# Graph attention with running sums in SBUF, no DMA in the edge loop but the gathers, and the sums first in each of TensorE's slots

## The chip, the cores and the metric

The kernel runs on one core of one Trainium2 chip. The metric is the time of the program on the device in microseconds (us), the median of some runs. All times of the profile come from one profiled execution.

## The reference

The inputs are 6250 nodes of 256 features and 200000 edges; `dst` is sorted, and since it is drawn as 6250 times the square of a uniform number, the edges are dense at low nodes and thin at high ones. Cut to what matters:

```python
# graph attention on xn = layernorm(x)
proj = (xn @ Wp.T).reshape(-1, 8, 32)
s = sum(proj * a_src)[src] + sum(proj * a_trg)[dst]
s = leaky_relu(s, 0.2)
s = s - max(s)
exp_s = exp(s)
denom = segment_sum(exp_s, dst)
out = segment_sum(proj[src] * exp_s / (denom[dst] + 1e-16), dst)
x = x + elu(out + xn @ Wskip.T + bias)
# top-2 of 8 experts with a hidden width of 1024, on layernorm(x)
x = x + sum over the two experts of weight * (gelu(xe @ W1 + b1) @ W2 + b2)
```

## The kernel before

The program has six stages, one after the other: `edge_tables` (indices of the edges turned so that an edge lies on each partition), `node_phase` (normalized, projected rows of all nodes, written to a table in DRAM), `edge_phase` (the edge loop, which this change is about), `route_phase` (attention output, router, tokens scattered by expert), `expert_phase` and `combine_phase`.

**The edge loop.** The sorted edges are taken in sub-tiles of 128, 4 sub-tiles in a **set** (512 edges), 2 sets in a **step**. There are 392 sets: 98 iterations of a loop body with 4 sets, u = 0 to 3. All edges of a step go to a window of 128 nodes that starts at the step's first target (`base_tab`). Where a step spanned more, the whole loop would be run once more (`over_passes`); with these inputs there is one pass. A **slot** is what each engine does for one set. For set u:

- GpSimd gathers, in four indirect DMAs (`rows[k]`, line 555), the table row of each edge's source: 256 projected features, 8 source scores, 8 target scores.
- VectorE compares (line 625): it writes `onehot[k]`, for each edge the one-hot row of its node in the window.
- TensorE turns the one-hots (`turn`, four fp32r matmuls against an identity, line 574), ScalarE copies them from PSUM (`onehot_t`, line 714), and TensorE multiplies them with the target scores of the window's nodes (`target_scores`, four fp32 matmuls of 9 columns, line 582). This gives each edge its target's score in the bank `z[k]`; the ninth column, of ones, tells which edges are in the window.
- VectorE adds source and target score (`add`, lines 634 and 637), ScalarE takes the exponential twice: as a factor in PSUM (line 718) and into the last 8 columns of `weighed`. VectorE multiplies the gathered rows by the factor (`weigh`, line 643).
- TensorE sums over edges by node (`sums`, four fp32 matmuls of one-hots by `weighed`, 264 columns, line 592) into a PSUM bank that is shared by the two sets of a step. After the step VectorE adds the bank to `accbuf` (`accumulate`, line 659).

A matmul of fp32 operands is issued as two instructions, so `sums` is 8 and `target_scores` 8, `turn` 4.

**The running sums** lie in DRAM (`acc_rows`). For each step SyncE loads the 128 rows of its window into `accbuf`, and stores them when the step has been added. A window's load waits for the store of the one before, as the windows overlap. SyncE also loads the window's 128 by 8 target scores (`st_w`) out of the table. `acc_rows` is cleared in the first stage and read again in `route_phase`.

**What sets the order.** No scheduler: each engine runs the instructions in the order in which its own function is written, and semaphores connect them. TensorE's slot u is `turn(u+2)`, `sums(u)`, `target_scores(u+2)`; VectorE's is `add(u)`, `weigh(u)`, `compare(u+2)`, then `accumulate` or `largest` (the running maximum of the exponentials, lines 650 and 654); ScalarE's is the exponentials of u, the copy of the indices, and `copy_turned(u+2)`. There are 4 buffers of rows, one-hots, `weighed` and `z`, and one bank for the turned one-hots. A gather into `rows[k]` waits for the weighing of the set before in the same buffer (`weigh_done[k]`).

## Time and profile before

| what | value |
| --- | --- |
| median of 3 runs | 3961.45 us (3962.35, 3954.32, 3961.45) |
| profiled execution, its own time | 3958.48 us |
| profiled execution, span | 3956.9 us |
| granted clock of TensorE, mean | 0.735 of full speed |
| TensorE (PE) busy | 2792.9 us, 71% |
| weight loads (PEld) busy | 2407.7 us, 61% |
| VectorE (DVE) busy | 1816.3 us, 46% |
| GpSimd (POOL) busy | 1746.9 us, 44% |
| ScalarE (ACT) busy | 874.4 us, 22% |

The span is from the first to the last recorded instruction. Busy shares are means over all stages: by the windows of the trace the edge loop is from about 227 to 2811 us, 65% of the span; the stage of tables ends at about 30 us, routing at about 3158 us. A matmul's end is modelled in the records: a TensorE instruction can be drawn as ended while the engine that waits for it goes on waiting.

### The profile page before, as it was taken

The numbers are of one execution on the slowest core, as the hardware profiler recorded it, in microseconds if no ns is written. First come the engines' busy times: TensorE is split into PE (matmuls) and PEld (weight loads), VectorE is DVE, ScalarE is ACT, GpSimd is POOL, SyncE is SP. The second block draws the span as 40 slices with busy tenths as digits, with TensorE's granted clock in tenths as the row PEclk, the third lists the DMA queues.
The fourth block names the chain that finished last, engine by engine and source line by source line (L and its number), as shares of the span: only waits on it lengthen the run. The fifth ranks groups of instructions, "written<-read, shape, count | busy, mean of one in ns | idle before, by whom it ended". The sixth has DMA issues, their size and how long they took to land. (4 is left out here: it accounts for less than half of the span.)

```text
span 3956.9 us, 52520 instructions
## 1 busy us (share of the span) xinstructions
PE 2792.9 (71%) x14065; PEld 2407.7 (61%) x14066; DVE 1816.3 (46%) x4809; ACT 874.4 (22%) x2715; POOL 1746.9 (44%) x1828
## 2 busy tenths in 40 slices
PE   5766777687777777777787778777303439999991
PEld 4445666566666656666666667566302339999991
DVE  5533434343443333343344434343576546666654
ACT  2211111111111111111111111111101225555540
POOL 0045555555555555555555556555103632221210
PEclk8977767766776776777767666667655569999995
DMA  4333333333333333333333334333332242221216
GB/s 149 113 104 104 106 105 108 102 109 103 105 105 105 106 108 106 106 103 109 104 109 108 107 107 110 101 104 106 95 114 64 68 121 68 66 86 45 65 45 200
DMA packets 256279, 400.63 MB, mean 101 GB/s; under 512 B 76674, under 2 KB 187739, under 8 KB 255625
## 3 DMA queue, kind: packets, MB, share of 16 engines
q0 software_dynamic: 98560, 262.95, 24.2%
q1 hardware_dynamic: 138165, 117.93, 9.7%
q10 hardware_dynamic: 19540, 19.60, 1.5%
q8 instruction: 4, 0.07, 0.0%
q14 instruction: 10, 0.08, 0.0%
HBM read 318.49 MB, written 81.71 MB: 101 GB/s over the span
## 5 line engine op out<-in xcount | busy, mean ns | idle before, releaser
L555 POOL DMA_INDIRECT rows<-proj_table,idx x1568 | 1482.2, 945 | 1312.7 <-DVE weighed L643 548.3
L592 PE MATMUL banks<-weighed,onehot 128*128 128x264 f32 x3136 | 1186.1, 543 | 0.0
L592 PEld LDWEIGHTS banks<-weighed,onehot 128*128 128x128 f32 x3136 | 827.3, 277 | 177.8
L582 PEld LDWEIGHTS banks<-st_w,onehot_t 128*128 128x128 f32 x3152 | 550.9, 254 | 618.1 <-ACT onehot_t L714 435.5
L582 PE MATMUL banks<-st_w,onehot_t 128*128 128x9 f32 x3152 | 534.6, 298 | 494.8 <-ACT onehot_t L714 383.3
L643 DVE TENSOR_TENSOR weighed<-rows,banks 128x1024 f32<-128x1024 f32 x392 | 478.7, 1221 | 560.8 <-ACT banks L718 370.7
L714 ACT COPY onehot_t<-banks 128x512 f32<-128x512 f32 x394 | 230.9, 586 | 2143.3 <-remote 1418.3
L574 PE MATMUL banks<-ident_r,onehot 128*128 128x128 f32 x1576 | 355.4, 364 | 146.9 <-DVE onehot L625 99.4
L634 DVE TENSOR_TENSOR raw_score<-rows,banks 128x32 f32<-128x32 f32 x392 | 73.1, 186 | 730.2 <-remote 501.5
L574 PEld LDWEIGHTS banks<-ident_r,onehot 128*128 128x128 f32 x1576 | 296.1, 264 | 168.5 <-DVE onehot L625 114.5
L1368 POOL DMA_INDIRECT results_by_token<-yrow,goes_to x104 | 108.6, 1044 | 479.2 <-DVE yrow L1316 350.1
L625 DVE SCALAR_TENSOR_TENSOR onehot<-banks,base_tab,dst_tab 128x512 fp32r<-128x512 f32 x394 | 293.5, 745 | 0.0
L1255 ACT ACTIVATE hid<-banks,params 128x256 f32<-128x256 f32 x416 | 198.0, 478 | 268.0 <-PE banks L1211 261.5
L1211 PE MATMUL banks<-f_xth,w1h 128*128 128x256 f32 x832 | 236.2, 284 | 28.5 <-ACT hid L1255 14.6
L1110 POOL DMA_INDIRECT tokens_by_expert<-r_xn,slot x100 | 118.1, 1181 | 278.8 <-issue 233.7
L1304 DVE TENSOR_TENSOR hidl<-hid,hidh 128x256 fp32r<-128x256 f32 x416 | 169.9, 424 | 149.4 <-ACT hidh L1249 138.3
L1211 PE MATMUL banks<-f_xth,w1l 128*128 128x256 f32 x832 | 234.1, 281 | 0.0
L1211 PE MATMUL banks<-f_xtl,w1h 128*128 128x256 f32 x832 | 234.0, 281 | 0.0
L659 DVE TENSOR_TENSOR accbuf<-accbuf,banks 128x264 f32<-128x264 f32 x197 | 83.8, 425 | 242.5 <-remote 198.5
L1211 PEld LDWEIGHTS banks<-f_xth,w1h 128*128 128x128 f32 x832 | 158.2, 190 | 32.5 <-issue 16.4
L1224 PE MATMUL banks<-w2h,hidh 128*128 128x256 f32 x832 | 170.4, 286 | 0.0
L1224 PE MATMUL banks<-w2l,hidh 128*128 128x256 f32 x832 | 166.1, 281 | 0.0
(214 smaller groups left out, 2860.6 us busy)
## 6 DMA issues: line engine op xcount, KB each, us to landing
accbuf<-acc_rows SPq DMA_DIRECT2D x197, 132.0 KB
acc_rows<-accbuf SPq DMA_DIRECT2D x197, 132.0 KB
rows<-proj_table,idx POOLq DMA_INDIRECT x1568
w_raw<-in_L_ffn_W_dram POOLq DMA_DIRECT2D x16, 1024.0 KB
xrow<-tokens_by_expert SPq DMA_DIRECT2D x106, 128.5 KB
c_y<-results_by_token SPq DMA_DIRECT2D x10, 1120.0 KB
proj_table<-trow ACTq DMA_DIRECT2D x50, 132.8 KB
acc_rows<-clear SPq DMA_DIRECT2D x5, 1320.0 KB, 13.1
```

What stands on the lines that cost most here:

```text
L555: nc.gpsimd.indirect_dma_start(rows[k][:, i, :], None, table, bass.IndirectOffsetOnAxis(ap=idx[k][:, i:i + 1], axis=0)).then_inc(gathered[ ...
L574: mm = nc.tensor.matmul(turn_bank[:, i * P:(i + 1) * P], onehot[k][:, i, :], m["ident_r"][:], start=True, stop=True)
L582: mm = nc.tensor.matmul(z[k][:, i, :], onehot_t[k % 2][:, i * P:(i + 1) * P], st_w[k // 2][:], start=True, stop=True)
L592: mm = nc.tensor.matmul(acc_bank[k // 2][:, 0:ROW], onehot[k][:, i, :].bitcast(F32), weighed[:, k * SET + i, :], start=(k % 2 == 0 and i = ...
L625: nc.vector.scalar_tensor_tensor(onehot[k][:], node_row.unsqueeze(1).to_broadcast(shape), m["base_tab"][:, bass.ds(2 * it + ahead // 2, 1) ...
L643: nc.vector.tensor_tensor(weighed[:, k * SET:(k + 1) * SET, 0:D].rearrange("p s (h f) -> p s h f", h=H), rows[k][:, :, 0:D].rearrange("p s ...
L714: nc.scalar.copy(onehot_t[k % 2][:], turn_bank[:]).then_inc(turn_copied[k], 1)
L1110: nc.gpsimd.indirect_dma_start(xg, bass.IndirectOffsetOnAxis(ap=slot[u][k][:], axis=0), xn[:, u, k, :], None).then_inc(sent[u], 16)
L1211: mm = nc.tensor.matmul(h_bank[j % HB][:, 0:TOK], w[:, s, k, at], v[:, k, :], start=(k == 0 and n == 0), stop=(k == KD - 1 and n == 2))
L1224: mm = nc.tensor.matmul(y_bank[h][:, 0:D], v[:, j, h * P:(h + 1) * P], w[:, s, j, :], start=(j == 0 and n == 0), stop=(j == JH - 1 and n = ...
L1255: nc.scalar.activation(hid[:, j, :], h_bank[j % HB][:, 0:TOK], ACT.Gelu, bias=params[:, s, B1 + j:B1 + j + 1]).then_inc(h_ready[j % HB], 1)
L1304: nc.vector.tensor_tensor(hidl[:, j, :], hid[:, j, :], hidh[:, j, :].bitcast(F32), ALU.subtract).then_inc(hid_low, 1)
```

## The change

The sums and the target scores stay in SBUF for the whole loop.

- `acc` is now a tile of 125 partitions by 52 node tiles by 264 columns, zeroed by GpSimd in the first stage. Windows are 125 nodes wide, so a window touches two neighbouring node tiles. `accumulate` (line 751) makes two VectorE instructions for a step: the bank times a 0/1 column (`upper`) added to the one node tile, and times the other column (`nextt`) to the next one. Which tile, a table says (`tile_int`), from which VectorE reads 7 registers in an iteration.
- Target scores are kept as three bf16 parts of 8 columns in `st_parts`, made at the end of `node_phase`. `pick` (lines 705 and 708) puts the 24 columns of a window together in two VectorE instructions for each step; `target_scores` is four bf16 matmuls of 24 columns (line 647), and a new VectorE instruction, `reduce` (line 713), adds the three parts of each score from PSUM to SBUF.
- `turn` (line 637) reads the upper halves of the fp32 one-hots as bf16, so it is four bf16 matmuls; there are two turn banks, two `z` banks, four `onehot_t` and eight `onehot`.
- `compare` (line 695) needs one table in place of two: `key_tab`, each edge's place in the window, is worked out ahead for all edges in the first stage (`find_keys`), with `inside_tab`, which says which edges are in the window and takes the place of the column of ones.
- An iteration has 8 sets, so there are 49. TensorE's slot u is now `sums(u)`, `turn(u+4)`, `target_scores(u+2)`. VectorE's is `add(u)`, `reduce(u+1)`, `pick` (even u) or `accumulate` (odd u), `compare(u+5)`, `weigh(u)`, and `largest` (odd u). ScalarE copies set u+3.
- The table's rows are 264 words long, not 272. The DRAM buffer `acc_rows`, its clearing, all of SyncE's loads and stores in the loop, and the loads of the sums in `route_phase` are gone. After a pass `next_windows` works out the keys of the next pass (`find_keys` again), even after the last one.

```diff
-SET, K = 4, 4
+SET = 4
 G = 2 * SET
+ROUND = 8
+STEPS_A_ROUND = ROUND * SET // G
+BUF = 4
...
-STEPS = 2 * -(-NSUB // (2 * G))
-IT = STEPS // 2
+STEPS = STEPS_A_ROUND * -(-NSUB // (STEPS_A_ROUND * G))
+IT = STEPS // STEPS_A_ROUND
+AHEAD = 3
...
-TROW = ROW + H
-ZC = H + 1
-ACC_TILES = -(-(N + P) // P)
...
+PARTS = 3
+ZC = PARTS * H
...
-            acc=sb("acc", [NP, NT, ROW]), neg_bound=sb("neg_bound", [P, 1]),
+            acc=sb("acc", [NP, NT + 2, ROW]), neg_bound=sb("neg_bound", [P, 1]),
...
+def find_keys(nc, m, step, settle):
+    def by_step(t):
+        return t[:, 0:(STEPS + AHEAD) * G].rearrange("p (s g) -> p s g", g=G)
+    key, inside = m["key_tab"], m["inside_tab"]
+    step(nc.vector.tensor_tensor(by_step(key), by_step(m["dst_tab"]),
+                                 m["base_tab"][:].unsqueeze(2).to_broadcast([P, STEPS + AHEAD, G]), ALU.subtract))
+    settle()
+    step(nc.vector.tensor_scalar(inside[:], key[:], 0.0, None, ALU.is_ge))
+    settle()
+    step(nc.vector.scalar_tensor_tensor(inside[:], key[:], float(NP), inside[:], ALU.is_lt, ALU.mult))
+    settle()
+    step(nc.vector.scalar_tensor_tensor(key[:], m["place_tab"][:], 1.0, inside[:], ALU.add, ALU.mult))
...
+            nc.gpsimd.memset(m["acc"][:], 0.0)
...
+            for to, op in ((m["upper"], ALU.is_le), (m["nextt"], ALU.is_gt)):
+                step(nc.vector.tensor_scalar(to[:, 1:1 + STEPS + AHEAD], first[:], m["iota_p"][:], None, op))
+                step(nc.vector.tensor_scalar(to[:, 0:1], first[:, STEPS - 1:STEPS], m["iota_p"][:], None, op))
...
+            targets = m["dst_tab"][:, 0:(STEPS + AHEAD) * G]
+            whole_parts(m["inside_tab"][:], targets, m["key_tab"][:])
...
+            step(nc.vector.scalar_tensor_tensor(m["place_tab"][:], m["inside_tab"][:], -float(NP), targets,
+                                                ALU.mult, ALU.add))
+            find_keys(nc, m, step, settle)
...
+            parts = [m["st_parts"][0:NP, 0:NT, q * H:(q + 1) * H] for q in range(PARTS)]
+            nc.vector.tensor_copy(parts[0], st_all[:]).then_inc(st_step, 1)
+            dve.wait_ge(st_step, 1)
+            nc.vector.tensor_tensor(st_rest[:], st_all[:], parts[0], ALU.subtract).then_inc(st_step, 1)
+            dve.wait_ge(st_step, 2)
+            nc.vector.tensor_copy(parts[1], st_rest[:]).then_inc(st_step, 1)
+            dve.wait_ge(st_step, 3)
+            nc.vector.tensor_tensor(parts[2], st_rest[:], parts[1], ALU.subtract)
...
-        onehot, onehot_t = tiles("onehot", [P, SET, P], F32R), tiles("onehot_t", [P, SET * P], n=2)
...
+        onehot, onehot_t = tiles("onehot", [P, SET, P], n=ROUND), tiles("onehot_t", [P, SET * P], BF16)
+        onehot16 = [o[:].bitcast(BF16).rearrange("p s (e half) -> p s e half", half=2)[:, :, :, 1] for o in onehot]
+        ident16 = sb("ident16", [P, P], BF16)
...
+            def turn(s, copied, compared):
+                if copied is not None:
+                    pe.wait_ge(turn_copied[(s - 2) % BUF], copied)
+                pe.wait_ge(onehot_ready[s % BUF], compared)
                 for i in range(SET):
...
+                    mm = nc.tensor.matmul(turn_bank[s % 2][:, i * P:(i + 1) * P], onehot16[s % ROUND][:, i, :],
+                                          ident16[:], start=True, stop=True)
+                mm.then_inc(turned[s % BUF], 1)
+            def target_scores(s, count, read):
+                pe.wait_ge(turn_copied[s % BUF], count)
+                pe.wait_ge(st_ready[s // 2 % 2], count)
+                if read is not None:
+                    pe.wait_ge(reduced[(s - 2) % BUF], read)
                 for i in range(SET):
...
+                pe.wait_ge(weigh_done[k], weighed_count)
                 for i in range(SET):
...
+                    mm = nc.tensor.matmul(acc_bank[u // 2 % 2][:, 0:ROW], onehot[u][:, i, :],
+                                          weighed[:, k * SET + i, :], start=(u % 2 == 0 and i == 0),
+                                          stop=(u % 2 == 1 and i == SET - 1), skip_group_check=True)
                 mm.then_inc(sum_done[k], 1)
...
-                for u in range(K):
-                    ahead = (u + 2) % K
-                    turn(ahead, now if u < 2 else nxt)
-                    sums(u, now, nxt)
-                    target_scores(ahead, now if u < 2 else nxt, now16 if u < 2 else nxt16)
...
+                at = counts(pe, c, 3)
+                for u in range(ROUND):
+                    sums(u, at(u), at(u + 4))
+                    turn(u + 4, at(u + 2), at(u + 4))
+                    target_scores(u + 2, at(u + 2), at(u))
...
+            def compare(s, it, free):
+                if free is not None:
+                    dve.wait_ge(sum_done[s % BUF], free)
                 shape = [P, SET, P]
...
+                nc.vector.tensor_tensor(
+                    onehot[s % ROUND][:], node_row[s % 2].unsqueeze(1).to_broadcast(shape),
+                    m["key_tab"][:, bass.ds(ROUND * SET * it + s * SET, SET)].unsqueeze(2).to_broadcast(shape),
+                    ALU.is_equal).then_inc(onehot_ready[s % BUF], 1)
+            def pick(s, it, tile_of, count):
+                q, b = s % 2, s % BUF
+                col = STEPS_A_ROUND * it + 1 + s
+                st = [m["st_parts"][:, bass.ds(t, 1), :].rearrange("p a k -> p (a k)") for t in (tile_of, tile_of + 1)]
+                nc.vector.tensor_scalar(st_pick[q][:], st[1], m["nextt"][:, bass.ds(col, 1)], None, ALU.mult
+                                        ).then_inc(st_picked[q], 1)
+                dve.wait_ge(st_picked[q], count)
+                nc.vector.scalar_tensor_tensor(st_w[b][:], st[0], m["upper"][:, bass.ds(col, 1)], st_pick[q][:],
+                                               ALU.mult, ALU.add).then_inc(st_ready[q], 1)
+            def reduce(s, count):
+                dve.wait_ge(z_ready[s % BUF], count)
+                nc.vector.tensor_reduce(target[s % BUF][:], z_parts[s % 2], X, ALU.add).then_inc(reduced[s % BUF], 1)
...
+            def accumulate(q, col, tile_of, summed, before):
                 dve.wait_ge(sum_done[2 * q + 1], summed)
...
+                dve.wait_ge(acc_added[1 - q], before)
+                for side, t in ((m["upper"], tile_of), (m["nextt"], tile_of + 1)):
+                    to = m["acc"][:, bass.ds(t, 1), :].rearrange("p a d -> p (a d)")
+                    ins = nc.vector.scalar_tensor_tensor(to, acc_bank[q][0:NP, 0:ROW], side[0:NP, bass.ds(col, 1)], to,
+                                                         ALU.mult, ALU.add)
+                ins.then_inc(acc_added[q], 1)
...
+                at = counts(dve, c, 4)
+                landed = [value_of(dve, 16 * SET * (2 * it + q + 1)) for q in range(2)]
+                tile_of = tiles_of_steps(STEPS_A_ROUND * it, 7)
+                for u in range(ROUND):
+                    add(u, at(u), landed[u // BUF])
+                    reduce(u + 1, at(u + 5))
                     if u % 2:
...
+                        accumulate((u - 3) // 2 % 2, STEPS_A_ROUND * it + (u - 1) // 2, tile_of[(u - 1) // 2],
+                                   at(u + 2), at(u - 1))
                     else:
...
+                        pick(u // 2 + 2, it, tile_of[u // 2 + 3], at(u + 4))
+                    compare(u + 5, it, at(u + 1))
+                    weigh(u, at(u))
+                    if u % 2:
+                        largest(u, it, at(u), at(u + 1))
...
+            def copy_turned(s, count):
+                act.wait_ge(z_ready[s % BUF], count)
+                act.wait_ge(turned[s % BUF], count)
+                nc.scalar.copy(onehot_t[s % BUF][:], turn_bank[s % 2][:]).then_inc(turn_copied[s % BUF], 1)
...
-                    sp.wait_ge(z_ready[2 * j + 1], now)
-                    load_scores(j, ahead)
-                    sp.wait_ge(acc_added[1 - j], nxt if j else now)
-                    store(1 - j, done)
-                    sp.wait_ge(acc_stored, value_of(sp, 16 * (2 * c + j + 1)))
-                    load(j, here)
...
```

TensorE in the body of the edge loop, slot 0 before; `banks` are PSUM banks, and "x3" stands for the three matmuls that follow the first with the same operands:

```order
L574 MATMUL banks<-ident_r,onehot2 128x128 [waits onehot_ready2]
L574 MATMUL banks<-ident_r,onehot2 128x128 x3
L592 MATMUL banks<-weighed,onehot0 128x264 [waits weigh_done0,exp_ready0,acc_added0]
L592 MATMUL banks<-weighed,onehot0 128x264 x3
L582 MATMUL banks<-st_w1,onehot_t0 128x9 [waits st_loaded1,turn_copied2]
L582 MATMUL banks<-st_w1,onehot_t0 128x9 x3
```

The same slot of TensorE with the change:

```order
L658 MATMUL banks<-weighed,onehot0 128x264 [waits weigh_done0,exp_ready0,acc_added0]
L658 MATMUL banks<-weighed,onehot0 128x264 x3
L637 MATMUL banks<-ident16,onehot4 128x128 [waits onehot_ready0,turn_copied2]
L637 MATMUL banks<-ident16,onehot4 128x128 x3
L647 MATMUL banks<-st_w1,onehot_t2 128x24 [waits reduced0,st_ready1,turn_copied2]
L647 MATMUL banks<-st_w1,onehot_t2 128x24 x3
```

The turn has moved behind the sums, and is for the set four ahead; the scores are still those of the set two ahead, behind the same sums.

VectorE in the same body, before, from the accumulation of slot 0 to the end of slot 1:

```order
L659 TENSOR_TENSOR accbuf1<-accbuf1,banks 128x264 [waits acc_loaded1,sum_done3]
L634 TENSOR_TENSOR raw_score1<-rows1,banks 128x32 [waits gathered1,z_ready1]
L636 REGISTER_ALU
L637 SCALAR_TENSOR_TENSOR score1<-raw_score1 128x32 [waits added]
L643 TENSOR_TENSOR weighed<-rows1,banks 128x4x256 [waits factor_ready1]
L625 ISA [waits sum_done3]
L625 SCALAR_TENSOR_TENSOR onehot3<-banks,base_tab,dst_tab 128x512
L650 TENSOR_TENSOR masked<-weighed,banks 128x64 [waits exp_ready1]
L654 TENSOR_TENSOR runmax<-runmax,masked 128x64 [waits maxed]
```

And VectorE's slot 1 with the change:

```order
L719 TENSOR_TENSOR raw_score1<-rows1,target1 128x32 [waits gathered1,reduced1]
L722 SCALAR_TENSOR_TENSOR score1<-raw_score1 128x32 [waits added1]
L713 TENSOR_REDUCE target2<-banks 128x32 [waits z_ready2]
L751 ISA [waits acc_added0,sum_done3]
L751 SCALAR_TENSOR_TENSOR acc<-banks,upper,acc 125x264
L751 ISA
L751 SCALAR_TENSOR_TENSOR acc<-banks,nextt,acc 125x264
L695 ISA [waits sum_done2]
L695 TENSOR_TENSOR onehot6<-banks,key_tab 128x512
L729 TENSOR_TENSOR weighed<-rows1,banks 128x4x256 [waits factor_ready1,sum_done1]
```

The weighing of set 1 was the third instruction of its slot and waited for set 1's own scores alone; now the reduction of set 2, with its wait for set 2's scores (`z_ready2`), the accumulation and the comparison stand ahead of it in VectorE's queue.

## Rows read from the trace of the kernel before

**Rows 1.** Windows by stage: us, then each engine's busy us (instructions), granted clock, DMA share, GB/s

```profile
227.00:2796.00 2569.00, 1927.52 (x7778) 1606.14 (x7779) 1019.93 (x2144) 430.41 (x1563) 1481.35 (x1568) 0.70 0.39 106
2811.00:3158.00 347.00, 78.01 (x372) 64.41 (x371) 218.87 (x878) 50.52 (x113) 94.82 (x81) 0.50 0.28 86
```

**Rows 2.** Groups of the whole run: busy us, mean ns of one, idle before it and what ended that

```profile
L555 POOL DMA_INDIRECT rows<-proj_table,idx x1568 | 1482.2, 945 | 1312.7 <-DVE weighed L643 548.3 <-issue 536.5 <-ACT idx L710 227.8
L592 PE MATMUL banks<-weighed,onehot 128*128 128x264 f32 x3136 | 1186.1, 543 | 0.0
L643 DVE TENSOR_TENSOR weighed<-rows,banks 128x1024 f32<-128x1024 f32 x392 | 478.7, 1221 | 560.8 <-ACT banks L718 370.7 <-issue 190.1
```

**Rows 3.** Line 634 alone, first and last start in us

```profile
L634 DVE TENSOR_TENSOR raw_score<-rows,banks x392: 173/188/190, 236.6 to 2804.3; 128x32 f32<-128x32 f32 x196
```

**Rows 4.** Timeline of TensorE: start us, us, instruction, idle before and its releaser

```profile
1540.00 2.00 PE L592 MATMUL banks<-weighed,onehot 128*128 128x264 f32 x8
1541.83 0.96 PE L582 MATMUL banks<-st_w,onehot_t 128*128 128x9 f32 x8
1543.75 0.66 PE L574 MATMUL banks<-ident_r,onehot 128*128 128x128 f32 x4 [0.96 <-issue]
1544.25 1.99 PE L592 MATMUL banks<-weighed,onehot 128*128 128x264 f32 x8
1551.81 0.38 PE L582 MATMUL banks<-st_w,onehot_t 128*128 128x9 f32 x1 [5.57 <-ACT onehot_t L714]
```

**Rows 5.** Timeline of VectorE in the same stretch

```profile
1543.85 0.23 DVE L654 TENSOR_TENSOR runmax<-runmax,masked 128x64 f32<-128x64 f32 x1
1551.12 0.19 DVE L634 TENSOR_TENSOR raw_score<-rows,banks 128x32 f32<-128x32 f32 x1 [7.03 <-remote]
```

**Rows 6.** Timeline of GpSimd, last gather before its pause

```profile
1547.58 0.95 POOL L555 DMA_INDIRECT rows<-proj_table,idx  x1 [0.30 <-issue]
```

**Rows 7.** Timeline of TensorE at the lower granted clock

```profile
1553.92 1.11 PE L574 MATMUL banks<-ident_r,onehot 128*128 128x128 f32 x4 [0.24 <-DVE onehot L625]
1554.84 3.83 PE L592 MATMUL banks<-weighed,onehot 128*128 128x264 f32 x8
1558.46 0.86 PE L582 MATMUL banks<-st_w,onehot_t 128*128 128x9 f32 x4
```

**Rows 8.** Timeline of VectorE behind the last gather

```profile
2798.74 1.22 DVE L643 TENSOR_TENSOR weighed<-rows,banks 128x1024 f32<-128x1024 f32 x1 [0.46 <-ACT banks L718]
2802.19 1.22 DVE L643 TENSOR_TENSOR weighed<-rows,banks 128x1024 f32<-128x1024 f32 x1 [0.85 <-ACT banks L718]
```

**Rows 9.** Timeline of TensorE, bf16 matmuls of the routing stage

```profile
3023.02 0.25 PE L1087 MATMUL banks<-mask,lower 125*125 125x8 bf16 x1
3023.12 0.25 PE L1087 MATMUL banks<-before,ones 125*125 125x8 bf16 x1
```

**Rows 10.** Groups of VectorE, shapes apart, for prices

```profile
L893 DVE TENSOR_TENSOR att<-acc,den 125x512 f32<-125x512 f32 x25 | 17.3, 693 | 3.6
L1419 DVE SCALAR_TENSOR_TENSOR c_mid<-c_y,weights,acc 125x256 f32<-125x256 f32 x50 | 20.7, 480 | 39.3 <-DMA c_y<-results_by_token 39.3
L223 DVE TENSOR_REDUCE base_tab<-banks 128x196 f32<-128x392 f32 x1 | 0.6, 566 | 3.3 <-PE banks L260 3.3
L701 DVE TENSOR_REDUCE edge_top<-runmax 128x1 f32<-128x64 f32 x1 | 0.2, 210 | 0.0
L901 DVE TENSOR_SCALAR low<-att 125x512 f32<-125x512 f32 x25 | 10.7, 426 | 0.8
```

**Rows 11.** Timeline of VectorE, last step of the edge tables

```profile
30.12 0.15 DVE L240 COPY dst_tab<-dst_tab 128x16 f32<-128x16 f32 x1
```

**Rows 12.** Timeline of VectorE, start of the routing stage

```profile
2817.68 0.23 DVE L888 TENSOR_SCALAR den<-acc,eps 125x16 f32 x1 [3.61 <-DMA acc<-acc_rows]
2824.64 0.69 DVE L898 TENSOR_TENSOR att<-att,r_skin 125x512 f32<-125x512 f32 x1 [5.53 <-DMA r_skin<-skip_rows]
```

381 lines of the change are left out of this document (175 added, 206 removed).

## The prediction

> **What bounds the kernel now.** I read the windows by stage first [rows 1]: the edge loop fills most of the run, TensorE is its busiest engine (1927.5 of 2569 us), GpSimd next (1481.4) and VectorE third (1019.9). The groups [rows 2] give the largest items: 1568 gathers of 945 ns, 3136 instructions of the sums of 543 ns, 392 weighings of 1221 ns. Line 634 alone [rows 3] gives the pace: its 392 starts run from 236.6 to 2804.3, so (2804.3 − 236.6) / 391 = **6.57 us a set**. Four gathers are issued 945 + about 300 ns apart [rows 2, 6], 5.0 us a set, so GpSimd is not full.
>
> TensorE's timeline shows the four parts of a slot at both levels of its clock. [...] The mean granted clock of the loop is 0.70 [rows 1], and yet the pace is that of the lower clock. The reason shows in the stretch at full clock: TensorE's scores start at 1541.83 and its sums again at 1544.25 [rows 4], but VectorE waits from about 1544.1 to 1551.12 for its next scores [rows 5], and TensorE itself from 1546.2 to 1551.81 for a turned one-hot [rows 4]; both come 3.5 to 4.2 us after GpSimd began the last gather that it could issue, at 1547.58 [rows 6]. So while gathers run, TensorE's results are given out later than its records draw them. Behind the last gather two weighings are 3.45 us apart [rows 8]: without gathers the same program runs nearly twice as fast. The loop is bound by TensorE, with results at about the pace of the lower clock whatever the records say.
>
> **The change, part by part.** *The cycle.* TensorE's slot u becomes sums(u), turn(u+4), scores(u+2); VectorE's has reduce(u+1) ahead of weigh(u). Now reduce(u+1) waits for scores(u+1), which TensorE issues behind sums(u−1), which wait for weigh(u−1). So in every slot: weigh(u−1) ends, TensorE does sums, turn and scores, then VectorE does reduce, pick or accumulate, compare and weigh(u), and only then the next sums start. Before, the scores issued in slot u were first needed in slot u+2, two slots of slack; now it is one, and the two engines take turns.
>
> TensorE's half at the lower clock: sums 3.62 [rows 7]; turn, now bf16, 4 instructions; the only bf16 matmuls in a row lie 0.10 us apart at clock 0.50 [rows 1, 9], but are of 8 columns. [...] Sum **4.62**. At the full clock: 1.83 + 0.21 + 0.41 = 2.45.
>
> VectorE's half: reduce of 128x96 to 32, between 210 ns for 64 elements and 566 ns for 392 [rows 10]: 0.25. Even slots: pick, two instructions of 24 columns, as the smallest step costs 0.15 to 0.17 each [rows 3, 11], 0.35; compare 128x512, between 426 and 693 ns [rows 10], 0.61; weigh 1.22 [rows 2]: 2.45. Odd slots: accumulate, two scalar_tensor_tensor of 264 columns, 480 ns for 256 columns from SBUF [rows 10], 0.445 each, with a bank as source, 0.89; then 2.95. Mean **2.70** (ends 2.4 and 3.1). Two handoffs from engine to engine I take at 0.09 together (ends 0, and the 0.24 idle behind a compare in rows 7 for each). Cycle: 4.62 + 2.70 + 0.09 = **7.41 us** at the lower clock, 2.45 + 2.70 + 0.09 = **5.24** at the full one; 5.0 is GpSimd's floor.
>
> Everything else in the slot has cover by this: the exponentials, the copy of the turned one-hots (for u+3, a slot of slack), add(u), the 7 registers that VectorE loads in an iteration. Gathers of 264 instead of 272 words: DMA share is 0.39 [rows 1], nothing. The loads and stores of the window's sums: no wait for them shows in the loop's pace, so 0, at most what rows 12 show for such a load, 3.61, if it were late in some of 196 steps; they go anyway.
>
> *Ahead of the loop.* Tables: eight VectorE steps over 1592 columns. Scaled by columns from 426 ns of tensor_scalar and 693 of tensor_tensor for 512 [rows 10] they would take 1.3 and 2.2 at most; a part of each is fixed, so I take 1.0 and 1.8: 4 × 1.0 + 4 × 1.8 = 11.2, with small ones +14 (the last table step is now at 30.12 [rows 11]). Four steps of 400 columns at the node phase's end: +2. The zeroing of `acc` runs on GpSimd beside loading and turning: 0. *Behind it.* Keys worked out once more, +5, since only part of it is covered by the wait for GpSimd. Routing: the first tile no longer waits 3.61 for its sums and the 5.53 for the next loads [rows 12] may come up to 4.4 earlier, −8; for the waits of later tiles I take −4 (ends 0 and −10): −12. Sum **+9**.
>
> *The sum.* 391 × (7.41 − 6.57) = +328 to +330, and +9: 3958.5 + 339 = 4297 us. The profiled execution lasted 3958.5, 3.0 below the median; that is less than the error of any term, so I give it as it stands.
>
> [...] Here the granted clock was 0.70 with TensorE busy three quarters of the loop and 0.50 in routing, where it is busy 78 of 347 us [rows 1]; the new loop would have it busy 62% at the lower clock, in between. [...] The trace's own 0.70, were it kept, would put 40% of the time at the full clock, which is rival B.
>
> **The rivals.**
>
> *A, full clock and results on time: faster.* Bf16 turn and scores leave TensorE half of its instructions besides the sums, VectorE's rests let it be idle, and the late results seen before might belong to fp32r turns or to a queue that never empties. Then a set costs 5.24: 391 × (5.24 − 6.57) = −520, +9 → **3448 us**. For it: rows 8, where 3.45 is reached without gathers, and granted clock 1.0 in rows 4. Against it: late results came exactly with gathers, which stay, and a TensorE that rests more has not had a higher clock (routing: 0.50).
>
> *B, the share of the clock stays 0.70, results on time.* A mean of 0.70 between 0.5 and 1.0 is 40% of the time at full clock. Sets per us are then 0.4 / 5.24 + 0.6 / 7.41 = 0.157, one in 6.36 us: 391 × (6.36 − 6.57) = −82, +9 → **3886 us** (3750 to 4000). It passes from slower to faster where the full clock's share goes over about 0.3 of the time.
>
> *C, results are held until gathers pause: slower still.* In rows 5 and 6 the result came 3.5 us after the last gather's start. If in the new cycle scores come only then: the first gather starts some 0.8 us after a weighing (taken between an issue of 0.30 and a gather's 1.25), the fourth 3 × 1.25 later at 4.55, results come at 8.0, and VectorE's 2.7 follow: 10.7 us in place of 7.41. If that is so in one slot of six to one of three: 391 × 3.3 / 6 = +215, to +430 → **4510 to 4730 us**. For it: such holds in rows 4 to 6. Against it: at the lower clock results come on time [rows 7].
>
> *D, the change doesn't do what it says:* a step whose window is read wrongly would start a second pass and double the loop. The change keeps one pass by the same condition, so no chance of weight.
>
> *The main case* (its own range 4100 to 4450, from cycles of 6.9 to 7.8) has no extra hold and the lower clock in nearly all slots. It is slower than before from a cycle of 6.55 on.
>
> **How the numbers follow.** Main case 0.46, A 0.18, B 0.19, C 0.17. The prediction is the main case's 4297 us. The range reaches from A, 3450 (half of A's chance lies below it), to 4560, which leaves out most of C: together about 0.2 is out. About 0.2% (8 us) is what a measurement of this kernel can tell from none. Faster: A's 0.18 and 0.12 of B, 0.30. Within 0.2%: 0.02, what of B lies around no change. Slower: main case, C and 0.05 of B, 0.68.
>
> **What would show it.** In the profile after: line 719's starts 7.4 us apart; VectorE's reduce (line 713) with the largest idle time ahead of it, released by TensorE; the sums (line 658) waiting for VectorE's weighed (line 729); TensorE busy some 60% of the loop at a clock near 0.5; gathers in fours with a pause of over 2 us. The pace of the loop's start says which case it is: 5.2 is A, 6.4 B, over 8 C. Stage ends: tables at 44, the loop starting 16 us later, routing 12 shorter. Wrong would be: the reduce without a wait (the cycle isn't there), the sums waiting for PSUM or for gathers (GpSimd would be the bound), or VectorE's half far from 2.7.

## The result, and the profile after

The kernel with the change takes **4086.35 us** (median of 4 runs, 4084.52 to 4091.23) against 3961.9 for the kernel before beside it: 1.0331 times as long, 95% interval 1.0312 to 1.0351. That is 124 us slower; 4297 us was forecast, 335 slower. The sign and the mechanism were right, the size was not.

A series is a batch of executions that were taken together. In later series the change hardly moved, while the kernel before did; every experiment below is therefore told with the kernel before of its own series:

| series | kernel before, us | change, us | ratio, 95% interval |
| --- | --- | --- | --- |
| first | 3961.9 | 4086.35 | 1.0331 [1.0312, 1.0351] |
| second | 3347.65 | not run | |
| third | 3917.07 | 4087.84 | 1.0419 [1.0393, 1.0445] |
| fourth | 3352.45 | not run | |
| fifth | 3977.52 | 4089.64 | 1.0287 [1.0249, 1.0325] |
| sixth | 3347.96 | 4072.16 | 1.2166 [1.2146, 1.2186] |

The series with the kernel before near 3350 us have traces of other kernels, but none of the kernel before itself with its four gathers. The chip's number doesn't tell the two kinds of series apart: it is 3 both in the third series (3917) and in the sixth (3348).

Windows by stage of the change, the edge loop and the routing (columns as in [rows 1]: PE, PEld, DVE, ACT, POOL, granted clock):

```profile
253.00:2936.00 2683.00, 1521.52 (x6240) 1156.47 (x6240) 1224.17 (x3127) 469.34 (x1564) 1478.40 (x1563) 0.66 0.29 79
2956.00:3290.00 334.00, 76.40 (x369) 62.92 (x369) 215.68 (x871) 50.49 (x113) 95.70 (x81) 0.50 0.24 69
```

TensorE is busy 1521.5 us of the loop, 1927.5 before [rows 1], and rests 43% of it. Line 719 alone (the first addition of each set, which answers to [rows 3]):

```profile
L719 DVE TENSOR_TENSOR raw_score<-rows,target x392: 177/184/193, 252.9 to 2936.1; 128x32 f32<-128x32 f32 x196
```

(2936.1 − 252.9) / 391 = **6.86 us a set** against 6.57. The groups name the two waits that take turns:

```profile
L658 PE MATMUL banks<-weighed,onehot 128*128 128x264 f32 x3136 | 1345.2, 601 | 1167.8 <-DVE weighed L729 945.3 <-issue 222.5
L713 DVE TENSOR_REDUCE target<-banks 128x32 f32<-128x96 f32 x393 | 101.1, 257 | 1301.5 <-PE banks L647 883.3 <-issue 398.1 <-remote 20.1
L751 DVE SCALAR_TENSOR_TENSOR acc<-banks,upper,acc 125x264 f32 x197 | 97.0, 492 | 1.1 <-issue 1.1
```

The sums stood 0.0 us idle before [rows 2]; now TensorE is idle for 1167.8 us ahead of them, 945.3 of it put down to the weighing. VectorE is idle for 1301.5 us ahead of the reduction, 883.3 of it put down to the scores. The rest, called "issue" and "remote", has no release on record in this trace, in which some of the signals' records are missing. In the sixth series, where VectorE's signals are all there, the change has 1142.3 us ahead of the sums, all put down to the weighing, and 1285.5 ahead of the reduction, all put down to the scores. One slot shows both, in the timeline (start, us, engine, line) of a stretch at the lower clock:

```profile
1519.31 3.86 PE L658 MATMUL banks<-weighed,onehot 128*128 128x264 f32 x8 [3.00 <-issue]
1522.96 0.63 PE L637 MATMUL banks<-ident,onehot 128*128 128x128 bf16 x4
1523.39 0.31 PE L647 MATMUL banks<-st_w,onehot_t 128*128 128x24 bf16 x4
1523.73 0.26 DVE L713 TENSOR_REDUCE target<-banks 128x32 f32<-128x96 f32 x1 [1.52 <-issue]
1523.98 0.23 DVE L705 TENSOR_SCALAR st_pick<-st_parts,nextt 128x24 bf16 x1
1524.55 0.69 DVE L695 TENSOR_TENSOR onehot<-banks,key_tab 128x512 f32<-128x512 f32 x1
1525.15 1.21 DVE L729 TENSOR_TENSOR weighed<-rows,banks 128x1024 f32<-128x1024 f32 x1
1526.51 3.86 PE L658 MATMUL banks<-weighed,onehot 128*128 128x264 f32 x8 [2.81 <-DVE weighed L729]
```

Sums, turn and scores run from 1519.31 to about 1523.7, VectorE's reduce, pick, compare and weigh from 1523.73 to 1526.4, and the next sums start at 1526.51: 7.20 us for this slot. Beside TensorE's half VectorE has only the running maximum and the additions of the next set, under 1 us together, and TensorE has next to nothing beside VectorE's half.

Not all slots are so long. From the start of each weighing, I measured the time to the next reduction and from there to the next weighing, and sorted the 380 slots of the loop by the granted clock in TensorE's half: in 140 slots TensorE's half lies wholly at the lower clock (granted 0.50), and they take 7.30 us; over all 380 the mean clock in TensorE's half is 0.585, and the mean slot 6.84. Where the full clock goes is seen best in the sixth series, where every slot of the loop has the same division. Windows over TensorE's half, VectorE's half, and the same again, of the change there:

```profile
1499.40:1502.85 3.45, 3.41 (x16) 2.54 (x14) 0.00 (x1) 0.33 (x3) 2.73 (x3) 0.60 0.26 67
1502.85:1505.81 2.96, 0.00 (x1) 0.03 (x1) 2.95 (x6) 0.55 (x1) 1.05 (x2) 0.96 0.37 104
1505.81:1509.74 3.93, 3.89 (x16) 2.96 (x16) 0.61 (x4) 0.65 (x4) 2.67 (x3) 0.60 0.23 56
1509.74:1512.52 2.78, 0.01 (x1) 0.04 (x1) 2.57 (x7) 0.55 (x1) 1.11 (x2) 0.98 0.40 114
```

Here TensorE has a clock of 0.60 while it works and 0.96 to 0.98 while it rests: in shorter windows of the first of these slots the clock is 0.50 from 1499.40 to 1501.80, in the sums, 1.00 from 1502.40 to 1504.50, and 0.50 again from 1505.81, where the next sums start. From 400 to 2300 us the turn, behind the sums, lies at the full clock in each of its 278 slots. The mean over this loop is 0.75, and it says nothing of the speed of the sums.

### The profile page after: what moved, and what is told of

Same layout as the page of the kernel before. It is cut to its first block and busy times, and to the rows that moved or that the text cites. A ratio compares the mean times of both kernels' runs of the same rounds, so it can differ in the third digit from the quotient of the medians.

```text
span 4086.3 us, 48805 instructions
## 1 busy us (share of the span) xinstructions
PE 2386.5 (58%) x12497; PEld 1955.8 (48%) x12498; DVE 2050.1 (50%) x5824; ACT 914.4 (22%) x2716; POOL 1761.8 (43%) x1829
## 5 line engine op out<-in xcount | busy, mean ns | idle before, releaser
L658 PE MATMUL banks<-weighed,onehot 128*128 128x264 f32 x3136 | 1345.2, 601 | 1167.8 <-DVE weighed L729 945.3
L658 PEld LDWEIGHTS banks<-weighed,onehot 128*128 128x128 f32 x3136 | 887.6, 296 | 1400.7 <-issue 1195.5
L713 DVE TENSOR_REDUCE target<-banks 128x32 f32<-128x96 f32 x393 | 101.1, 257 | 1301.5 <-PE banks L647 883.3
L831 ACT CAST onehot_t<-banks 128x512 bf16<-128x512 f32 x395 | 231.4, 586 | 1023.1 <-PE banks L637 918.6
L836 ACT ACTIVATE banks<-score,neg_bound 128x32 f32<-128x32 f32 x392 | 114.1, 291 | 1200.8 <-DVE score L722 1172.5
L695 DVE TENSOR_TENSOR onehot<-banks,key_tab 128x512 f32<-128x512 f32 x397 | 270.4, 682 | 0.0
L637 PEld LDWEIGHTS banks<-ident,onehot 128*128 128x128 bf16 x1584 | 182.7, 137 | 137.6 <-issue 86.7
L637 PE MATMUL banks<-ident,onehot 128*128 128x128 bf16 x1584 | 224.8, 288 | 2.7 <-DVE onehot L695 2.7
L1293 PE MATMUL banks<-w2h,hidl 128*128 128x256 f32 x832 | 165.9, 281 | 0.0
L1318 ACT CAST hidh<-hid 128x256 fp32r<-128x256 f32 x416 | 161.3, 401 | 0.0
```

The source lines that it names most:

```text
L637: mm = nc.tensor.matmul(turn_bank[s % 2][:, i * P:(i + 1) * P], onehot16[s % ROUND][:, i, :], ident16[:], start=True, stop=True)
L658: mm = nc.tensor.matmul(acc_bank[u // 2 % 2][:, 0:ROW], onehot[u][:, i, :], weighed[:, k * SET + i, :], start=(u % 2 == 0 and i == 0), sto ...
L695: nc.vector.tensor_tensor(onehot[s % ROUND][:], node_row[s % 2].unsqueeze(1).to_broadcast(shape), m["key_tab"][:, bass.ds(ROUND * SET * it ...
L831: nc.scalar.copy(onehot_t[s % BUF][:], turn_bank[s % 2][:]).then_inc(turn_copied[s % BUF], 1)
L1293: mm = nc.tensor.matmul(y_bank[h][:, 0:D], v[:, j, h * P:(h + 1) * P], w[:, s, j, :], start=(j == 0 and n == 0), stop=(j == JH - 1 and n = ...
L1318: nc.scalar.copy(hidh[:, j, :], hid[:, j, :]).then_inc(hid_high, 1)
```

## The experiments

**The wait taken off the weighing.** VectorE's reduction moved behind the weighing, second series:

```diff
                     add(u, at(u), landed[u // BUF])
-                    reduce(u + 1, at(u + 5))
...
                         largest(u, it, at(u), at(u + 1))
+                    reduce(u + 1, at(u + 5))
```

> VectorE's reduce(u+1) stands behind weigh(u) and largest. Theory of the cycle (VectorE's reduce waits for scores that TensorE issues behind the sums of the set before, so the two engines take turns, 6.86 us a set): the wait no longer holds the weighing, the chain closes only over two sets (about 7 us for two), and GpSimd's gathers bound the loop at 5.0 to 5.3 us a set, so 3410 to 3500 us. Rival, late results (TensorE's results come about 3.5 us after the gathers pause, as before the change): the pace goes back to 6.3 to 6.6, 3870 to 3990 us.

Measured: 3361.24 us beside 3347.65 for the kernel before (ratio 1.0038 [1.0024, 1.0052]). The groups of it:

```profile
L713 DVE TENSOR_REDUCE target<-banks 128x32 f32<-128x96 f32 x393 | 98.2, 250 | 0.3 <-PE banks L647 0.3
L719 DVE TENSOR_TENSOR raw_score<-rows,target 128x32 f32<-128x32 f32 x392 | 75.3, 192 | 663.1 <-DMA rows<-proj_table,idx 663.1
```

The reduction waits 0.3 us in all, and VectorE waits for gathers instead; line 719 starts from 256.2 to 2213.4, 5.01 us a set, GpSimd's floor (four gathers of 945 ns, each with about 300 ns to the next, [rows 2, 6]). The cycle was real, and this one move opens it. The time lies under the expected 3410 to 3500, though the 5.0 us a set was right: by itself it gives 4086 − 391 × (6.86 − 5.0) = 3359, which the range should have reached. Against the kernel before it gains nothing here: that takes about the same time, 3347.65 us. With 5.0 us a set and all else as in its first trace, it would have a span of 3956.9 − 391 × (6.57 − 5.0) = 3343 us, so it is most likely at the same floor. That is an estimate, as this kernel has no trace in this series.

**The scores taken out from behind the sums.** The same cut at the other end, on TensorE:

```diff
                 for u in range(ROUND):
-                    sums(u, at(u), at(u + 4))
                     turn(u + 4, at(u + 2), at(u + 4))
                     target_scores(u + 2, at(u + 2), at(u))
+                    sums(u, at(u), at(u + 4))
```

> TensorE's slot is turn(u+4), scores(u+2), sums(u). Theory of the cycle: the reduce finds its scores done before the sums of the set before start, VectorE's wait is gone, GpSimd bounds the loop at 5.0 to 5.3 us a set, 3410 to 3500 us. Rival, late results: 6.3 to 6.6 a set, 3870 to 3990 us. Rival, the clock alone decides (the lower one for most of the sums): as with the change, within 1%.

Measured: 3362.66 us beside 3347.65, reduction without a wait, 5.0 us a set, again a little under the expected range. It is the order of `sums` and `target_scores`, and not the bf16 scores or the accumulation taken alone, that made the change slow.

**The turn alone ahead of the sums**, the order of the kernel before:

```diff
                 for u in range(ROUND):
-                    sums(u, at(u), at(u + 4))
                     turn(u + 4, at(u + 2), at(u + 4))
+                    sums(u, at(u), at(u + 4))
                     target_scores(u + 2, at(u + 2), at(u))
```

> TensorE's slot is turn(u+4), sums(u), scores(u+2), the parts in the order of the kernel before. Theory of the cycle: the four matmuls of the turn (0.4 us behind one another in the trace of the change) run in VectorE's half, and the scores stay behind the sums: 6.86 - 0.35 to 0.45 = 6.4 to 6.5 us a set, 3910 to 3950 us. Rival, the order of TensorE's parts matters only through its total work: no change, 4086 us within 0.5%.

Measured: 3984.49 us, a loop of 6.58 us a set. The expected 3910 to 3950 was missed. Of its 363 slots, 214 have TensorE's half wholly at the lower clock and take 6.86 us against 7.30 for the change: 0.44, which is the turn's four matmuls to about 10 ns (0.43 us from the first of them to the scores behind them, the mean of 189 slots of the change's first trace at clock 0.50). The mean fell by less, as its TensorE half had the full clock less often (mean 0.567 against 0.591 for the change in the sixth series).

**One accumulation instead of two** (the part of the sums that belongs to the next node tile is left out):

```diff
-                for side, t in ((m["upper"], tile_of), (m["nextt"], tile_of + 1)):
+                for side, t in ((m["upper"], tile_of),):
```

> The accumulation leaves out its second instruction (the part of the sums that belongs to the next node tile isn't added). Theory of the cycle: VectorE's half is on the path, so 0.40 us less in every second set, 0.20 a set, 391 x 0.20 = 78: 4000 to 4015 us. Rival, VectorE is idle over half of the loop and the instruction is covered: 4086 us within 0.3%.

Measured: 4038.88 us, 6.70 us a set; 48 us under the 4087 of the change in the other series where I had expected 78, and 33 under that of the sixth; the expected 4000 to 4015 was missed. At equal clock the slots are where they should be: 180 slots with TensorE's half wholly at the lower clock take 7.08 us, 0.22 less than 7.30. So VectorE's half is on the path. On average over all slots it is 0.20 to 0.21 shorter than in the change's traces of the sixth and first series, and TensorE's half, with the full clock a little less often, 0.05 to 0.08 longer: part of the gain is given back there.

**Both ends cut, in the third series,** where the kernel before took 3917; the edits are the first two above, together:

> TensorE's slot is turn, scores, sums, and VectorE's reduce stands behind the weighing. Theory: either change alone brought the loop to GpSimd's floor of 5.0 us a set (3361 and 3363 us), so both together give no more: 3355 to 3365 us. Rival, some of the waits that are left in those two add up: 3340 us or less.

Measured: 3992.81 us (ratio 1.0172 [1.0145, 1.0200] to the kernel before, 2.3% under the change in the same series). The expected 3355 to 3365, the floor of either cut alone, was missed by far: in this series most of what the cut cycle gave went to the next wait, TensorE's held results. Timeline:

```profile
1500.38 0.25 PE L647 MATMUL banks<-st_w,onehot_t 128*128 128x24 bf16 x4
1502.94 0.25 PE L647 MATMUL banks<-st_w,onehot_t 128*128 128x24 bf16 x4
1504.33 1.35 PE L658 MATMUL banks<-weighed,onehot 128*128 128x264 f32 x5 [1.13 <-DVE weighed L729]
1506.00 0.38 PE L658 MATMUL banks<-weighed,onehot 128*128 128x264 f32 x1 [0.33 <-issue]
1508.10 0.38 PE L658 MATMUL banks<-weighed,onehot 128*128 128x264 f32 x1 [1.72 <-issue]
1509.50 0.60 PE L658 MATMUL banks<-weighed,onehot 128*128 128x264 f32 x1 [1.02 <-issue]
1513.52 0.95 POOL L616 DMA_INDIRECT rows<-proj_table,idx  x1 [0.30 <-issue]
1516.55 0.26 DVE L713 TENSOR_REDUCE target<-banks 128x32 f32<-128x96 f32 x1 [12.37 <-remote]
```

The last three of the eight matmuls of one set of sums come out one at a time, 1.4 to 2.1 us apart, though nothing on record makes them wait, and the scores drawn as done at 1500.63 reach VectorE at 1516.55, 3.0 us after the last gather began. The late scores are what [rows 4 to 6] show, longer.

**The kernel before in the third series:**

> The kernel before, unchanged, for a trace from the chip on which the experiments run, since there it took 3348 us and not 3961. Theory of late results (the trace before showed TensorE's results come 3 to 9 us after their modelled end while gathers run): in this trace they come within 0.1 us of it, the gathers stand 1.25 us apart with little pause, 5.0 us a set. Rival, the granted clock: it was 0.70 in the loop and would be near 1.0 here. Rival, the gathers are faster here: under 945 ns each or closer than 1.25 us.

Measured: 3916.58 us, held results as in the first series, and not the results on time that were expected: this series was not like the second. I counted them in every trace: a group of matmuls whose signal comes over 0.5 us behind the modelled end of its last matmul, within the edge loop, its ends and the signals without a record left out.

| kernel | kernel before in its series | groups held |
| --- | --- | --- |
| before, first series | 3962 | 634 of 1008 (mean 4.2 us) |
| before, third | 3917 | 676 of 1003 |
| both orders, third | 3917 | 697 of 948 (mean 10.3 us) |
| change, first | 3962 | 2 of 954 |
| change, third | 3917 | 0 of 894 |
| change, fifth | 3978 | 1 of 983 |
| reduction last, scores first, turn first, one accumulation | 3348 | 0 of 1094 to 1116 each |
| change, sixth | 3348 | 0 of 1143 |

So holds are a state that a series has or has not. In such a series the kernel before meets them more at the full clock (482 of the 566 groups that ended there in its first trace), but not only there (152 of the other 442). The change is nearly free of them. A likely reason is that it never works long at the full clock, and the fillers below agree with that, but no run separates the clock from the rests.

**The change again:**

(The kernel of the change without an edit, three times.)

> The change, unchanged, on the chip of the experiments. Theory of the cycle (TensorE's half and VectorE's in turn, whatever the chip): 6.8 to 6.9 us a set, 4070 to 4100 us, so some 22% over the kernel before here. Rival, the chip makes everything faster: 3450 us.

> The change, unchanged. Theory of the cycle: 4070 to 4100 us whatever the chip, beside the kernel before at either 3350 or 3940. Rival, on a chip where the kernel before takes 3350 the change is faster than 4000.

> The change, unchanged. Theory of the cycle: 4070 to 4100 us, also if the kernel before stands near 3350 us here, which would be 22% slower than it. Rival, on such a chip it is faster than 4000.

Measured: 4087.84, 4089.64 and 4072.16 us, all as expected; what varies is the kernel before. Beside a kernel before without holds the change is 22% slower, beside one with holds 3 to 4%.

**Filling TensorE's rests.** Twenty bf16 matmuls that nobody reads, behind the scores, to keep TensorE at work in VectorE's half:

```diff
-                mm.then_inc(sum_done[k], 1)
+
+            def filler(u):
+                for _ in range(20):
+                    mm = nc.tensor.matmul(acc_bank[u // 2 % 2][:, 264:264 + P], ident16[:], ident16[:], start=True, stop=True,
+                                          skip_group_check=True)
+                mm.then_inc(sum_done[u % BUF], 1)
...
                     target_scores(u + 2, at(u + 2), at(u))
+                    filler(u)
```

They write beside the sums in the accumulating bank, each with the start mark. No instruction of the work is left out, but the kernel's output is changed, by a relative error of 0.14; what happens to the sums in the bank, no run separates. The signal that the sums are done goes out behind the fillers.

> Twenty bf16 matmuls that nobody uses stand behind the scores in each of TensorE's slots, 2.1 us at the lower clock, inside VectorE's half of 2.9 us; for that the signal that the sums are done goes out behind them. Theory of the clock (TensorE's half is long because its rests keep the granted clock at 0.5 to 0.6 there): the clock rises towards 1.0, TensorE's half falls from 4.0 to 2.3 us, 5.2 to 5.6 us a set, 3440 to 3620 us. Rival, the clock stays: 4086 us within 1%, or more if the fillers reach the next sums.

> The same kernel as filler (twenty unused bf16 matmuls in VectorE's half of each slot). If the kernel before stands near 3350 us here (no results held): theory that the rests of TensorE put the lower clock onto the sums: granted clock 1.0 in nearly all of the loop, 5.15 to 5.4 us a set, 3430 to 3530 us against some 4090 for the change. Rival, the clock falls back anyway: over 3900. If the kernel before stands near 3940: as filler, 4274 us, since results are held at the full clock.

> The same kernel as filler. If the kernel before stands near 3350 us here: theory that TensorE's rests put the lower clock onto the sums: granted clock 1.0 in nearly all of the loop, no results held, 5.15 to 5.4 us a set, 3430 to 3530 us. Rival: over 3900. If the kernel before stands near 3950: 4270 us again.

Measured: 4274.07 and 4269.46 us in the third and fifth series, **3579.25** in the sixth (the change there: 4072.16). Windows of the sixth, then of the fifth:

```profile
400.00:2300.00 1900.00, 1294.08 (x12312) 1090.67 (x12310) 1064.22 (x2735) 406.24 (x1364) 1292.80 (x1368) 0.94 0.36 97
```

```profile
400.00:2300.00 1900.00, 1135.37 (x9360) 921.77 (x9360) 809.47 (x2076) 311.12 (x1039) 986.60 (x1042) 0.83 0.28 74
```

In the sixth series the clock rose to 0.94; 289 of 360 slots lie wholly at the full clock and take 5.30 us, and the loop 5.55 ((2424.4 − 253.4) / 391). More work on TensorE made the loop 1.26 us a set faster (6.82 to 5.55), so TensorE's rests are what held its clock down. The range of 3430 to 3530 was missed since a fifth of the slots still met the lower clock. The first run of this kernel, in the third series, had missed its range of 3440 to 3620 for another reason: in the series with holds it had a higher clock than the change too (0.83 in the window above), but met the holds, 514 of 1075 and 548 of 1089 groups, and lost. One slot of the fifth series,

```profile
1512.62 1.00 PE L664 MATMUL banks<-ident 128*128 128x128 bf16 x15
1514.58 0.38 PE L664 MATMUL banks<-ident 128*128 128x128 bf16 x4 [0.96 <-issue]
1516.00 0.22 PE L664 MATMUL banks<-ident 128*128 128x128 bf16 x1 [1.04 <-issue]
1517.57 0.26 DVE L719 TENSOR_REDUCE target<-banks 128x32 f32<-128x96 f32 x1 [6.95 <-remote]
```

has matmuls a microsecond apart with nothing on record that they wait for.

**One gather of four,** for the kernel before, in a series without and in one with holds, and for the change. The rows of the other three sub-tiles stay zero, so most of the sums are left out, and the count that the wait asks for is cut to match:

```diff
-                    for i in range(SET):
+                    for i in range(1):
                         nc.gpsimd.indirect_dma_start(
...
+                nc.vector.memset(rows[k][:, 1:SET, :], 0.0)
```

> The kernel before with one gather of the four in a set; the rows of the other three sub-tiles stay zero, so most of the sums are left out. What decides is how the kernel before stands on the same chip. If it is near 3940 (TensorE's results held): theory that the gathers cause the holds: 3.4 to 4.5 us a set, 2720 to 3150 us, and holds (a result's signal over 0.5 us behind the modelled end of its matmuls) fall from 63% of the groups to under 20%. Rival, the full clock causes them, gathers or not: 3700 us or more, holds on most groups. If it is near 3350 (no holds): GpSimd was the bound at 5.0, and TensorE's or VectorE's work is next: 3.4 to 4.5 us a set again.

> The same kernel as before_one_gather. If the kernel before stands near 3350: 2792 us again. If near 3940: theory that the gathers beside the full clock cause the holds: holds on under 20% of the groups and 2790 to 3150 us. Rival, the full clock alone causes them there: holds on half of the groups, 3700 us or more.

> The change with one gather of the four in a set (the other sub-tiles' rows stay zero). Theory of the cycle (VectorE and TensorE in turn, the gathers covered): 6.7 to 6.9 us a set whatever the chip, 4030 to 4100 us. Rival, the gathers or their traffic are on the path: under 3700 us.

Measured for the kernel before: 2792.11 us in the fourth series and 2791.62 in the fifth, where the full kernel took 3977.52. Windows of the fifth:

```profile
400.00:1500.00 1100.00, 1027.31 (x6252) 917.47 (x6253) 794.95 (x1720) 352.02 (x1252) 296.39 (x313) 1.00 0.29 79
```

TensorE is busy 93% at a clock of 1.00, and not one of 1108 groups is held. So in a series with holds the full clock alone doesn't hold results; it takes the gathers beside it. What of the gathers does it, their transfers or GpSimd's issuing of them, is not separated. In a series without holds the two together hold nothing either: the kernel with the fillers in the sixth series has four gathers a set and a clock of 0.94, and none of its groups is held. For the change: 4101.47 us, a little over the expected 4030 to 4100, and (2922.3 − 256.8) / 391 = 6.82 a set with a quarter of the gathers, as with all of them in the sixth series. They are fully covered in the change.

**The two cuts again,** fourth and sixth series:

> The same kernel as scores_first. If the kernel before stands near 3350 us here: 3360 again. If near 3940: theory that the holds come whenever TensorE runs freely at the full clock with gathers beside it: 3850 to 4050 us, like both orders together (3993), though the chain over one set is cut. Rival, the holds came from something that both orders together add: 3360 us.

> The same kernel as reduce_last. As for scores_first_again: 3360 us where the kernel before is near 3350; where it is near 3940, by the theory of holds 3850 to 4050 us.

> The same kernel as reduce_last. If the kernel before stands near 3350 us: 3361 to 3368 again, the loop at GpSimd's floor. If it stands near 3950: theory of held results 3900 to 4050 us; rival, the cut chain alone frees the loop there too: 3370 us.

Measured: 3368.38 and 3366.02 us beside 3352.45, and 3362.18 beside 3347.96. Each series was one without holds, so what a single cut gives where there are holds stays open; both cuts together gave 3992.81 there. The version with the reduction last beats the change by 17% (3362.18 against 4072.16 in one series), but no version that I ran beats the kernel before: its loop is at the same floor, and the 16 us of longer tables are left.

## Why the prediction was right and wrong

- **The cycle** was right: reduce(u+1) waits for scores(u+1) behind sums(u−1) behind weigh(u−1). Two experiments show it by cutting it (4072 to 3362 us for the one in the same series), and two by shortening one half. 392 starts of line 719 are one pass, so rival D did not occur.
- **Its length at one clock** was right: 7.41 us forecast at the lower clock, 7.30 measured; 5.24 at the full one, 5.30 measured with the fillers. TensorE's half was 4.62 + 0.09 and came as 5.780 − 1.21 = 4.57, VectorE's 2.70 as 1.52 + 1.21 = 2.73. Of what is added up in 4.62 and in the 2.45 for the full clock, no run of the kernel before shows the turn's 0.43 and 0.21 or the scores' 0.57 and 0.41. In the change's first trace the turn took 0.43 us up to the scores at clock 0.50 (189 slots) and 0.22 at 1.00 (89 slots), and the scores are drawn with 0.31 and 0.25. The sums' 3.62 and 1.83 are in [rows 7] and, from 1540.00 to 1541.83, in [rows 4]; they measured 3.65 in the change (95 slots) and 1.86 with the fillers of the sixth series (274 slots), each up to the turn. The 0.445 for an accumulation out of a bank, below the 480 ns of [rows 10], was an estimate too; in the change's first trace the two start 0.41 us apart and take 0.89 together (mean of 197).
- **The step that failed** is the main case's "the lower clock in nearly all slots". Its term, TensorE's half at 4.62 in every slot, measured 5.31 − 1.21 = 4.10 on average, as the full clock reached into part of it (0.585). The cycle came out at 6.86 in place of 7.41, and 391 × (7.41 − 6.86) = 215 is all of the error of 4297 − 4086 = 211. Of these 0.55 us a set, 0.44 is the clock (7.30 to 6.86) and 0.11 the two halves priced a little long (7.41 to 7.30). The sign that named the clock failed with it: near 0.5 was to be seen, and the loop had 0.66. That the lower clock would hold in nearly all slots was my estimate; no row of the trace before shows it for a loop of this kind.
- **The row that was left out.** For the clock the prediction leaned on the routing stage, whose bursts of 3.5 us and rests of mostly 3.5 to 4.7 stay at the lower clock throughout. The same trace had a stage that says otherwise and that the prediction left out. In the node phase TensorE is busy 67% of the time, nine in ten of its rests are under 1.2 us, and the clock is 0.92. The rests of 2.7 us that were forecast for the new loop lie between the two, and so did its clock. The node phase, a stretch of routing, and two of routing's bursts (for each the idle time before it):

```profile
30.60:227.00 196.40, 131.35 (x519) 89.92 (x519) 94.24 (x432) 48.44 (x152) 0.00 (x0) 0.92 0.31 103
3000.00:3150.00 150.00, 71.10 (x340) 58.79 (x340) 87.94 (x525) 30.54 (x79) 89.87 (x77) 0.50 0.25 66
3030.24 0.27 PE L1087 MATMUL banks<-before,ones 125*125 125x8 bf16 x1 [3.52 <-DVE mask L976]
3037.84 0.27 PE L1087 MATMUL banks<-before,ones 125*125 125x8 bf16 x1 [4.08 <-DVE mask L976]
```

- **Rival B** had the clock's share (0.70 forecast, 0.66 measured) and missed too, at 3886: it spread the full clock evenly over the slot, and it falls on the rests (0.60 at work, 0.96 to 0.98 at rest in the sixth series). With the rests filled the clock of the loop was 0.94.
- **Rival C** did not occur: 2 held groups of 954. The reason given against it, that at the lower clock results come on time, holds for the change, but not for the kernel before, where 152 of 442 groups were held there.
- **Rival A** did not occur in the change, but its 5.24 is what a slot takes when the clock is full (5.30 in the fillers' trace of the sixth series).
- **"The loop is bound by TensorE"** was read rightly from the one trace, where at clock 0.50 turn, sums and scores take 0.92, 3.62 and about 1.7 (twice the 0.86 of four) [rows 7], 6.3 of the 6.57 us a set. It is not the kernel's nature: in three series of six the kernel before took 3350 us, which by the estimate above is GpSimd's 5.0 us a set. A baseline that sits in such a state makes a change look 3% slower that is 22% slower otherwise. The trace before had the hint, results late against their own records, and I used it only for a rival.
- **Ahead of the loop**: +16 forecast, 252.9 − 236.6 = +16.3. The eight large steps came as sized (0.99 and 1.82 each); the tables end at 47.8, not 44, and 3.7 of this is that the first reduction into `base_tab` starts at 31.19 where it started at 27.51 before, but the loop's start moved by no more than forecast. **Behind it**: 4086.3 − 2936.1 = 1150.2 against 1152.6, so −2.4 where −7 was forecast. Up to VectorE's `eps`, behind the keys of the next pass, it is 18.5 us from the last addition against 7.6 before, +11 where +5 was forecast; the rest came 13 shorter where 12 was forecast. The sum closes: the loop from first to last addition is 2683.2 − 2567.7 = 115.5 us longer, 115.5 + 16.3 − 2.4 = 129.4, and the spans differ by 4086.3 − 3956.9 = 129.4.

## What to carry to other kernels

When instructions change places in a queue, write down for each wait how many slots ahead its producer runs, and what the producer itself waits for. Where that distance was one slot here and both engines were in the loop, their times added up (4.57 and 2.73 in a slot of 7.30 us); moving one instruction behind another removed 710 us here (4072 to 3362 in one series) with the same work. Price a stretch of alternating work and rest at the clock of the working half, not at the mean (0.60 and 0.75 in the sixth series), and measure the baseline in more than one series before believing a difference of a few per cent.

## What the runs showed of the hardware that was not expected

- The full clock can fall almost wholly on an engine's rests: 0.60 at work, 0.96 to 0.98 at rest in a whole series, slot after slot. Useless matmuls in the rests took 12% off (4072 to 3579).
- With four gathers a set (106 GB/s in the loop of the kernel before [rows 1]) and TensorE at the full clock for much of the time (a mean of 0.70 there), results are held in three series: 634 of 1008 groups of the kernel before in the first, 676 of 1003 in the third, 548 of 1089 with the fillers in the fifth. One set's scores reached VectorE 15.9 us behind their modelled end (1500.63 to 1516.55, both orders), and matmuls of one group start up to 2.1 us apart there and up to 1.4 with the fillers of the third and fifth series. In the traces of the other three series no group is held. The kernel before took 3917 to 3978 us in the first kind and 3348 to 3352 in the other. With a quarter of its gathers no group was held in either kind.
- What sets this state stays open; the granted clock doesn't show it, and chip number 3 had both kinds. It leaves a second mark: the traces of the three series with holds lack some of the signals' own records. Of the signals that VectorE gives, the change's traces have 4412, 4359 and 4396 in the first, third and fifth series and 5198 in the sixth. The kernel before with one gather has 4445 in the fifth against 4667 in the fourth, with no group held in either. So the state touches the recording too, and a part of the recording in the holds isn't excluded: each execution on record, whose times are given here, has a recorded span, and none was timed without records.
